# Products that nobody reads in two waits of TensorE, in a gated delta layer with a mixture of experts

## The reference

```python
mixed = einsum('bth,ch->btc', hidden_states, qkv_w)
x = conv_general_dilated(mixed.T, conv_w, padding=[(3, 0)], feature_group_count=CONV_DIM)   # 4 taps
z = einsum('bth,vh->btv', hidden_states, z_w)
q, k, v = split(x.T, 3)
beta = sigmoid(bb); alpha = exp(-exp(A_log) * softplus(aa + dt_bias))
def step(S, inp):
    S = S * alpha_t
    kv = einsum('bhk,bhkv->bhv', k_t, S)
    S = S + einsum('bhk,bhv->bhkv', k_t, (v_t - kv) * beta_t)
    return S, einsum('bhk,bhkv->bhv', q_t, S)
o = o * rsqrt(mean(o * o) + EPS) * norm_w
o = o * (z * sigmoid(z))                       # the gate
out = einsum('btv,hv->bth', o, out_w)
...
logits = flat_x @ W_router + b_router          # top 2 of 8, softmax
h = relu(flat_x @ W1[e] + b1[e]); y = h @ W2[e] + b2[e]
final_output += y * w[:, e]
```

## Time and profile before

| what | us |
|---|---|
| median of 3 runs (1407.96 to 1409.8) | 1408.25 |
| the profiled execution | 1407.17 |
| its span, first to last instruction | 1405.3 |
| TensorE busy (matmuls) | 1172.5 |
| VectorE busy | 1167.0 |
| ScalarE busy | 834.4 |
| GpSimd busy | 710.7 |
| mean granted clock of TensorE | 0.933 |

### The profile page before, as it was taken

One profiled execution on the slowest core, in us unless ns is written; L12 is line 12 of the kernel. 1 busy time (PEld: TensorE's weight loads), 2 busy tenths in 40 slices (PEclk: granted clock), 3 DMA queues, 4 the chain that ended last, 5 costly groups with the idle time before them and its releaser, 6 DMA issues.

```text
span 1405.3 us, 33741 instructions
## 1 busy us (share of the span) xinstructions
PE 1172.5 (83%) x11978; PEld 944.4 (67%) x11978; DVE 1167.0 (83%) x2531; ACT 834.4 (59%) x2536; POOL 710.7 (51%) x598
## 2 busy tenths in 40 slices
PE   0355989898989899898989899999898988469992
PEld 0233868686868686777777777777777777358881
DVE  6878898988888889888888889898989894578875
ACT  1242666665666666666666656566665655348884
POOL 3151726465545555564646373828291914235552
PEclk9996999998989999999999999999999999789996
DMA  6031212222122222222212131313030314332225
GB/s 206 0 98 31 73 36 71 57 59 61 54 62 53 62 54 62 54 61 54 63 52 66 49 69 47 83 35 97 21 99 21 105 18 134 95 105 74 79 64 180
DMA packets 163174, 97.07 MB, mean 69 GB/s; under 512 B 115623, under 2 KB 148269, under 8 KB 161988
## 3 DMA queue, kind: packets, MB, share of 16 engines
q1 hardware_dynamic: 124932, 82.25, 21.5%
q10 hardware_dynamic: 33536, 4.20, 2.1%
q0 software_dynamic: 4544, 8.47, 1.9%
HBM read 73.31 MB, written 24.61 MB: 70 GB/s over the span
## 4 chain that ended last, share of the span: by engine, by line
DVE 32%; PE 26%; POOL 16%; issue 10%; DMA 7%; ACT 6%; SPq 2%; POOLq 0%; DVEq 0%; ACTq 0%
POOL kq L637 9%; DVE Y_sb L1056 7%; DVE blkT L1060 7%; PE kx L1541 3%; POOL decay L629 3%; POOL rows_in L609 2%; DMA blkN<-scr_n 2%; PE kx L1636 2%; POOL kq L620 2%; PE rc L1703 2%; DVE blkN L1047 2%; DVE Gs L1204 1%; DVE area L1146 1%; ACT Gs L836 1%; PE rc L1704 1%
## 5 line engine op out<-in xcount | busy, mean ns | idle before, releaser
L637 POOL TENSOR_TENSOR kq<-tapA,area 128x256 f32<-128x256 f32 x256 | 253.2, 1003 | 89.1 <-DVE area L1146 88.1
L758 ACT ACTIVATE area<-pj,taps 128x256 f32<-128x256 f32 x256 | 123.3, 482 | 138.8 <-PE pj L1555 130.4
L1056 DVE TENSOR_TENSOR Y_sb<-blkT,blkN 128x4 f32<-128x4 f32 (+18 forms) x304 | 172.4, 567 | 10.5
L1541 PE MATMUL kx<-kq 128*128 128x128 f32 x1024 | 143.1, 288 | 43.2 <-ACT area L767 32.6
L609 POOL DMA_INDIRECT rows_in<-rowbuf,dest x64 | 64.8, 1012 | 214.8 <-DVE dest L1132 187.3
L1541 PEld LDWEIGHTS kx<-kq 128*128 128x128 f32 x1024 | 130.2, 199 | 57.8 <-issue 41.2
L1143 DVE SCALAR_TENSOR_TENSOR tapA<-pj,taps,tapA 128x256 f32<-128x256 f32 x256 | 122.2, 477 | 51.7 <-ACT tapA L758 49.8
L620 POOL TENSOR_TENSOR kq<-kq,area 128x1024 f32<-128x1024 f32 x64 | 151.1, 2363 | 0.0
L1060 DVE TENSOR_REDUCE blkT<-Y_sb 128x2 f32<-128x4 f32 (+18 forms) x304 | 142.5, 469 | 5.2
L758 ACT ACTIVATE tapA<-pj,taps 128x256 f32<-128x256 f32 x256 | 123.1, 481 | 0.0
L1146 DVE SCALAR_TENSOR_TENSOR area<-pj,taps,area 128x256 f32<-128x256 f32 x256 | 121.4, 474 | 0.0
(11 more groups left out here) (305 smaller groups left out, 3593.6 us busy)
## 6 DMA issues: line engine op xcount, KB each, us to landing
area<-scr_alpha SPq DMA_DIRECT2D x32, 512.0 KB, 4.2
area<-scr_acum SPq DMA_DIRECT2D x32, 512.0 KB, 3.8
blkN<-scr_n SPq DMA_DIRECT2D x32, 256.0 KB, 4.3
area<-rows_in SPq DMA_DIRECT2D x39, 130.0 KB, 2.2
scr_n<-area SPq DMA_DIRECT2D x128, 32.0 KB, 1.6
area<-rows_out SPq DMA_DIRECT2D x4, 1024.0 KB, 8.0
rows_in<-rows_in SPq DMA_DIRECT2D x8, 260.0 KB, 3.8
kq<-in_x SPq DMA_DIRECT2D x4, 512.0 KB, 6.0
```

The costliest lines, as they stand in the source:

```text
L637: nc.gpsimd.tensor_tensor(dst[:, n % H, :], tapA[:, n % RING, :], tapB[:, n % RING, :], ALU.add).then_inc(conv_done, 1)
L758: ins = nc.scalar.activation(dst[:, n % RING, :], pj[n % 2][:, k:k + GT], ACT.Copy, scale=taps[:, t, k:k + 1])
L1056: ins = nc.vector.tensor_tensor(p4, bc(blkT[:, r0:, j:].rearrange("p r (o m) -> p r o m", o=1), [128, nr, w, wd]), bc(blkN[:, j:j + w, j:] ...
L1541: ins = mm(o, lhs[:, hh, cs], rhs_[:, hh, cs], start=True, stop=True)
```

## The change

A table gives two steps, kq.0.1 and gt.0.0, a number of stand-in products, 7 and 8. Before either step, in every round that has both a group to finish and a group to prepare (15 rounds), TensorE waits as step z.0.0 would for its bank, then multiplies a 128x128 piece of the f16 value weights by a 128x512 piece of the same weights, that many times, into bank pj[0]. Each product starts its sum anew and signals nothing. The bank's next use is z.0.0, which also starts anew. All other steps and their order stay.

```diff
@@ -1422,6 +1422,11 @@
             for t in (xt_mm, logit_mm, place_mm):
                 pe.sem_inc(t, 1)
 
+            STAND_INS = {
+                ("kq", 0, 1): (("z", 0, 0), pj[0], 7),
+                ("gt", 0, 0): (("z", 0, 0), pj[0], 8),
+            }
+
             def bank_free(use, g, a, r=None):
 
                 uses = BANK_USES[bank_of(*use)]
@@ -1450,6 +1455,13 @@
                     if sure:
                         return
                     waited = waited or not late
+
+            def stand_in(step, g, a, r):
+
+                use, bank, n = STAND_INS[step]
+                bank_free(use, g, a, r)
+                for _ in range(n):
+                    mm(bank[:, :], wv_hi[:, 0, 0:C], wv_hi[:, 0, 0:512], start=True, stop=True)
 
             def merge(g, a, r, c, hop):
 
@@ -1644,6 +1656,8 @@
                         ins.then_inc(out_mm, 1)
 
                 for step, *arg in STEPS:
+                    if g is not None and a is not None and (step, *arg) in STAND_INS:
+                        stand_in((step, *arg), g, a, r)
                     if r is not None:
                         route(step, r, g, a)
                     if g is not None:
```

## The result

The changed kernel takes 1396.95 us (median of 4, 1396.63 to 1399.73), beside 1409.03 for the kernel before in the same comparison: a ratio of 0.9913, with a 95% interval of 0.9898 to 0.9929. A second comparison on another occasion gave 1397.01 us and 0.9900 (0.9882 to 0.9918). The prediction was 1396.5.

The account below looks back on a forecast made before the run. Bound: a chain across engines, with VectorE waiting before L1094 on TensorE's low clock. 10.95 us (14 rounds) plus 0.8 (first round) gave 11.8 off the profiled 1407.17: 1395.4, plus 1.1 for the median: 1396.5, range 1393.5 to 1405.

Parts of the forecast that it names:

- The bound: Before L1094 in the loop: the low clock costs VectorE's wait there, 0.78 us a round, 10.95 us in 14 rounds.
- a fall at the merges: Rival: the low clock moves to the 32x32 merges, behind the inverses' transfer; 1.7 us each, 7% chance.
- the 11.8: Whole kernel: forecast gain in us, 10.95 from 14 rounds plus 0.8 from the first round.
- The cover: Before kq.0.1 and gt.0.0: added products, 1.5 and 1.7 us a round, fit waits that ScalarE ends and cost nothing.
- Cushions of 0.6 and 0.7 us: Before kq.0.1 and gt.0.0: time left between the end of the added products and the step's start.
- The logits had 0.8 us in hand: Before L1094: with the clock high the logits stand 0.8 us before VectorE ends its earlier work.
- The first round: Round without routing: VectorE's 0.85 us wait at L1176 for a gate tile's tanh shrinks, gaining 0.8 us.
- TensorE would be over 2 us earlier there: First round, gate tiles before L1176: reason given for taking 0.8 us out of the possible 0 to 0.85.
- The last group's fall unchanged: Last group, where nothing is added: the clock's fall there was to stay as before, an expected sign without a gain.
- The fall among the transposes: Rival: the clock falls later, among the transposes behind gt.0.0; gain only 3.6 us, 1404.6 us, 8% chance.
- another end as late: Rival: VectorE's wait before L1094 has another equally late end, an ACT copy for instance; 1408 us, 5% chance.
- The clock falling all the same: Rival: the clock falls at 731 despite the products, gt.0.0 1.0 us late in 15 rounds; 1423 us, 4% chance.

Follow-up runs that it names:

- double: Changed kernel with 14 and 16 stand-in products in place of 7 and 8; ratio 1.0063 to the kernel before.
- twelve: Changed kernel with 12 products before gt.0.0 in place of 8, the 7 kept; 1399.00 us, ratio 0.9930 to the kernel before.
- merge_only: Kernel before with only 4 products added before the first merge m.1.0; 1408.27 us, ratio 0.9984 to the kernel before.
- small: Changed kernel with each added product cut to 16 columns; 1432.13 us against 1432.88 for the kernel before on that chip, ratio 0.9993.
- first_only: Changed kernel without the 8 products before gt.0.0, the 7 before kq.0.1 kept; 1402.76 us, ratio 0.9946 to the kernel before.
- turns: Changed kernel with 14 and 16 f32 transposes in place of the products; 1420.21 us, ratio 0.9899 to the kernel before (1432.9 on that chip).
- not_first: Changed kernel without its products in the first of the 15 rounds; 1398.51 us, ratio 0.9908 to the kernel before.

## Why the prediction was right

**The bound.** That VectorE's wait before L1094 is the price of the low clock, not TensorE's lost time, held: the 14 waits are gone, and the loop from the second round on is 10.9 us shorter, where the waits summed to 10.95. That the two agree to 0.1 us is luck: one more round with a fall at the merges put back about 1.6 us, and something else gave as much. VectorE's waits at L1176 and L1211 are part of it (1.5 us in the loop before, none after), but its waits for the blocks' transfer rose from 2.7 to 6.6 us, and its own instructions took 2.7 us less (819.2 before, 816.4 after), which no run explains. So I can't balance the account from the waits alone. The shortest round went from 67.94 to 67.03 us, 0.9 where one wait of 0.78 stood; the rest of that stays open. It is in part luck, too, that the median came within 0.5 us of the forecast: the profiled execution, the only one of the four whose parts can be read, gave 7.4 us of the 11.8, with nothing from the first round and 3.4 lost in the last group.

**The cover.** Cushions of 0.6 and 0.7 us were forecast, 0.41 and 0.80 measured. The logits had 0.8 us in hand by the forecast. In the round shown after the change they had 0.6: the logit products start at 727.28 and L1094 can follow 0.65 us behind, as before the change, at 727.93, while VectorE came at 728.52. `double` gives 0.8 (2.3 us late, 1.5 waited), and `twelve`, up to 0.7 us late, did not reach the end of it.

**The first round.** This term was mis-sized: 0.8 us forecast, -0.2 and -0.3 measured in the changed kernel's two traces, some 0.3 by the means over all kernels. The step that failed is "TensorE would be over 2 us earlier there": it was 1.6 us earlier at gt.1.0 (191.61, 193.25 before), and that lead did not last. In that stretch VectorE frees a bank, TensorE fills it, ScalarE takes its tanh and VectorE needs it; the wait at L1176 closes that ring, and a lead ahead of it mostly becomes waits of TensorE, for ScalarE and for L1176. That is argued from the code and the trace, where TensorE now waits 0.80 us for ScalarE's Gs (0.18 before) and 0.43 for L1176 (no wait before); no run tested it.

**The last group.** "The last group's fall unchanged" was wrong for the profiled execution: 3.4 us more. The falls at 1151 and 1165 were not in the trace before. The second profiled execution has one of them, at 1162.6, and lost 2.7 us there. But this is not shown to be a price of the change. `merge_only` and `small`, in whose loops the clock falls as before, took 59.8 and 62.6 us there, each with falls that the kernel before did not have between 1148 and 1200, and `first_only` took 57.3 with none between 1146 and 1196. The kernel before has one trace, and its 56.6 us is the shortest but one of the thirteen. Why the clock falls in some executions and not in others there was not tested.

**The rivals.** The fall among the transposes did not come, and in `turns` transposes held the clock in these two waits. Nor was another end as late. The fall at the merges did come more often in the first profiled execution, 2 rounds of the loop in place of 1, and once in the second; its price was put at 1.7 us and is 1.5 to 1.7 for a fall of 3.4 us, and 3.6 for the one of 6.8 in `first_only`. It stayed far from the 7 rounds that would have used up the gain. The clock falling all the same is what `small` shows, for another kernel.

## What to carry to other kernels

Look for stretches where TensorE's granted clock is low and ask who waits at their end; only that wait is to be had, here 0.78 us a round of the 1.9 us by which TensorE's work from gt.0.0 to the logits was longer at the low clock (4.70 us, and 2.80 after the change). Products without a reader, put into waits that another engine ends, cost nothing here while they ended before it did, nor when they ended later by less than what the next result had in hand (0.6 to 0.8 us). What went beyond that was paid in every round (1.5 us in `double`). So count them at the high clock and keep a few tenths of a us of room. When the low stretch is gone, look again at the other waits of the same engine, since the next one that lets the clock fall may lie there.

## What the hardware showed unexpectedly

In the two waits f32 transposes (16 in 1.9 us) held the clock at 1.00 as well as f16 products did. Fifteen products of 16 columns in the same places did not hold it. With only the second wait filled the clock fell in 8 rounds of 14, though the open wait was 1.93 or 1.94 us in each of the 14: whether a wait of this size lets the clock fall is not settled by its length alone. The waits for the transfer at the merges show the same: the clock fell behind 0.72 us of it in `turns` (405.9), and stayed high behind 1.45, 1.45 and 1.58 us in single rounds of the kernel before, `not_first` and `twelve`.
